# Attention and a ternary feed-forward on one core: first two batches without DMA transposes, weight loads on another queue, normalisations on GpSimd, a new table of times

## The reference

```python
# x, ctx: (16, 128, 1024)
x = x + tanh(g_xattn) * xattn(layernorm(x), ctx, ctx)
x = x + tanh(g_ffn) * ffn(layernorm(x))

def xattn(q, k, v):           # 8 heads of 64, per batch
    qh, kh, vh = Wq.T @ q, Wk.T @ k, Wv.T @ v        # (512, 1024)
    qh = softmax(qh, over a head's 64 rows) * 64 ** -0.5
    kh = softmax(kh, over the 1024 columns)
    context = kh @ vh.T        # 64 x 64 per head
    out = Wo @ (context.T @ qh) + bo
    return out / norm(out over the 128 rows) * g * sqrt(128)

def ffn(h):                    # h (2048, 1024), weights (2752, 1024)
    gate, up = h @ tern(w_gate).T, h @ tern(w_up).T
    return (gate * up) @ tern(w_down).T

def tern(w):                   # scale needs all of w first
    scale = mean(abs(w)); return round(clip(w / (scale + 1e-5), -1, 1)) * scale
```

## Time and profile before

| | us |
|---|---|
| median of 3 runs | 1525.23 (1522.23 to 1528.7) |
| the profiled execution | 1532.59 |
| its span, first to last instruction | 1530.7 |
| PE busy | 1356.5 (89%) |
| DVE busy | 948.4 (62%) |
| ACT busy | 643.7 (42%) |
| POOL busy | 313.7 (20%) |
| data moved by DMA | 196.41 MB |

### The profile page before, as it was taken

One profiled execution on the slowest core, in us unless ns is written; L12 is line 12 of the kernel. 1 busy time (PEld: TensorE's weight loads), 2 busy tenths in 40 slices (PEclk: granted clock), 3 DMA queues, 4 the chain that ended last, 5 costly groups with the idle time before them and its releaser, 6 DMA issues.

```text
span 1530.7 us, 23979 instructions
## 1 busy us (share of the span) xinstructions
PE 1356.5 (89%) x9596; PEld 960.9 (63%) x9596; DVE 948.4 (62%) x1495; ACT 643.7 (42%) x971; POOL 313.7 (20%) x233
## 2 busy tenths in 40 slices
PE   4546350978999999999999999999999999999999
PEld 2324220756757875687658765887578857884884
DVE  5777453766766776677676776676667675742220
ACT  4558663565524442434343443434344434330220
POOL 0129441163221112111121112121112121110000
PEclk9768675989999999999999999999999999999999
DMA  9897999977774246544752375435642565212001
GB/s 353 304 264 245 242 180 207 219 165 124 151 167 102 51 97 152 113 81 84 156 119 57 84 138 127 86 92 104 151 90 50 103 145 90 70 29 76 22 1 42
DMA packets 338191, 196.41 MB, mean 128 GB/s; under 512 B 304352, under 2 KB 304480, under 8 KB 338080
## 3 DMA queue, kind: packets, MB, share of 16 engines
q1 hardware_dynamic: 319120, 126.97, 40.9%
q10 hardware_dynamic: 18960, 67.90, 14.1%
HBM read 102.57 MB, written 16.78 MB: 78 GB/s over the span
## 4 chain that ended last, share of the span: by engine, by line
PE 79%; DMA 9%; DVE 5%; issue 4%; SPq 1%; ACT 1%; POOL 1%; ACTq 0%; DVEq 0%; POOLq 0%
PE ps L741 36%; PE ps L766 19%; PE ps L572 7%; PE ps L573 7%; PE ps L574 7%; DMA kT<-k 4%; DMA cx_raw<-in_ctxn 2%; DMA eT<-p 2%; PE ps L713 1%; SPq L512 1%; PE ps L721 1%; DMA qs<-in_wo 1%; DVE qs L1176 0%; DVE q_stat L1182 0%; DVE kT L949 0%
## 5 line engine op out<-in xcount | busy, mean ns | idle before, releaser
L741 PE MATMUL ps<-zT,w_gu 128*128 128x256 f16 x5504 | 626.2, 273 | 0.0
L741 PEld LDWEIGHTS ps<-zT,w_gu 128*128 128x128 fp8e4 x5504 | 539.5, 98 | 83.4
L766 PE MATMUL ps<-w_dn,inter_buf 128*128 128x512 fp8e4 x1376 | 307.7, 379 | 0.2 <-DVE inter_buf L949 0.2
L766 PEld LDWEIGHTS ps<-w_dn,inter_buf 128*128 128x128 f16 x1376 | 134.7, 99 | 154.2 <-issue 0.4
L1293 POOL TENSOR_TENSOR qs<-qs,q_stat 128x1024 f32<-128x1024 f32 x64 | 127.3, 1988 | 383.7 <-DVE q_stat L1187 383.7
L778 ACT ACTIVATE gate<-ps 128x256 f32<-128x256 f32 (+1 forms) x176 | 67.2, 382 | 310.2 <-PE ps L741 308.9
L1233 DVE SCALAR_TENSOR_TENSOR gate<-ps,gate 128x256 f32<-128x256 f32 (+1 forms) x176 | 74.0, 421 | 181.3 <-ACT gate L778 180.0
L949 DVE TENSOR_TENSOR inter_buf<-gate,inter_buf 128x256 f16<-128x256 f32 (+1 forms) x176 | 82.3, 467 | 66.9 <-ACT inter_buf L778 66.8
L572 PE MATMUL ps<-kT,cT 128*128 128x256 f16 x256 | 74.1, 289 | 52.1 <-DMA kT<-k 46.9
L889 ACT ACTIVATE qs<-qs,l_used 128x1024 f32<-128x1024 f32 x64 | 73.2, 1143 | 96.7 <-DVE qs L1176 96.7
L1299 POOL TENSOR_TENSOR rsv<-ssv,cst 128x4 f32<-128x4 f32 x32 | 45.4, 1418 | 323.6 <-DVE ssv L1203 323.6
(11 more groups left out here) (134 smaller groups left out, 1788.2 us busy)
## 6 DMA issues: line engine op xcount, KB each, us to landing
inter_buf<-in_gate_w ACTq DMA_DIRECT2D x20, 512.0 KB, 10.2
inter_buf<-in_up_w ACTq DMA_DIRECT2D x20, 512.0 KB, 5.7
w_dn<-in_up_w ACTq DMA_DIRECT2D x20, 512.0 KB, 6.0
w_dn<-in_gate_w ACTq DMA_DIRECT2D x19, 512.0 KB, 10.9
w_dn<-in_down_w ACTq DMA_DIRECT2D x18, 512.0 KB, 6.8
inter_buf<-in_down_w ACTq DMA_DIRECT2D x17, 512.0 KB, 5.1
cx_raw<-in_ctxn SPq DMA_DIRECT2D x16, 512.0 KB, 4.5
q_raw<-in_x SPq DMA_DIRECT2D x16, 512.0 KB, 4.7
```

The costliest lines, as they stand in the source:

```text
L741: last = nc.tensor.matmul(ps[:, j % 2, s * T:s * T + T], w_gu[:, w, k, :], zT[:, h, k, :], start=(k == 0 and h == 0), stop=(k == NC - 1 an ...
L766: mm = nc.tensor.matmul(ps[:, hf, :], lhs, w_dn[:, j, hf * 512:hf * 512 + 512], start=(u == 0), stop=(u == total - 1))
```

## The change

- For batches 0 and 1 the context is loaded a second time, already transposed in memory (`ld_ctxT`, an input `ctxt` that holds it so), and scaled and split on ACT and DVE (`ct_hi`, `ct_lo`) in place of `turn_c`; `z` is turned by PE (`zt`) and split out of PSUM (`zt_hi`, `zt_lo`) in place of `z_hi`, `z_lo`, `turn_z`.
- `wload` moves from ACT to SP; `ld_ctx`, `ld_xq`, `ld_xr` move from SP to ACT.
- A buffer `stage_c` of two slots is added, and a branch for slots above 10; `STAGES` itself is not in the diff.
- `q32`, `q_lo` and `z` move from DVE to POOL.
- The factor E_SCALE moves from a DVE instruction on the sums of q (`q_sized`) into the copies `e_hi`, `e_lo`, `qf_hi`, `qf_lo`.
- Of the sums of weights ACT takes four in five instead of two in three.
- `zT_in` becomes one semaphore for each batch of a group.
- All times of the table are new, with the second group now written out of its own. The chunks of down are summed from 1434 on instead of 1678.

```diff
-FFN_FROM = (1969, 3625, 5231)
-EVERY = 1607
+FFN_FROM = (1489, 3382, 5019, 6625)
+EVERY = 1606
...
-    "turn_c": [[159], [675], [1274], [1948], [2754], [3481], [-885], [-143]],
-    "kt": [[168, 181, 252, 265], [685, 709, 772, 792], [1284, 1504, 1517, 1635], [1909, 2075, 2088, 2161],
+    "ld_ctxT": [[0], [312], [], [], [], [], [], [], [], []],
+    "turn_c": [[], [], [1581], [2168], [2642], [3141], [3917], [4756], [-1088], [-276]],
+    "kt": [[139, 152, 201, 216], [558, 713, 833, 881], [1594, 1607, 1654, 1685], [2044, 2246, 2320, 2333],
...
-SUM_ACT = [c for c in range(IC) if c % 3 != 0]
+SUM_ACT = [c for c in range(IC) if c % 5 != 0]
...
+        stage_c = sb("stage_c", [P, 2, CH])
...
+            if s > 10:
+                return stage_c[rows, s - 11, cols]
...
-            def ld_ctx(i, _):
-                if i:
-                    wait(sp, c_lo_s, i)
-                    sp.dma_start(cx_raw[:, :], ctx_rows[rows_of(i), :]).then_inc(ctx_in, 16)
...
+            def wload(m, c, n):
+                kind = STAGED[n][0]
+                s = SLOT[n]
+                if n == 0:
+                    sp.wait_ge(ctx_in, 16)
+                wait_stage_done(sp, BEFORE[n])
...
+                    sp.dma_start(v, src[:, c * CH:c * CH + v.shape[1]]).then_inc(s_load_w[s], 16)
...
+            def zt(i, _):
+                if i == 0:
+                    pe.wait_ge(s_small, 80)
+                wait(pe, z_ready, i + 1)
+                wait_banks(proj_free[PROJ])
+                for k in range(NC):
+                    last = nc.tensor.transpose(ps[:, PROJ + k // 4, (k % 4) * P:(k % 4) * P + P],
+                                               z32[:, k * P:k * P + P], ident[:, :])
+                last.then_inc(zt_ready, 1)
+                proj_free[PROJ][0] = (zt_lo_s, i + 1)
...
+            def ld_ctx(i, _):
+                if i:
+                    wait(act, c_lo_s, i)
+                    nc.scalar.dma_start(cx_raw[:, :], ctx_rows[rows_of(i), :]).then_inc(ctx_in, 16)
...
+            def ld_xr(i, _):
+                if i < GB + BY_PE:
+                    wait(act, zt_ready, i - 1)
+                else:
+                    wait(act, zT_in[i % GB], 16 * ((i - BY_PE) // GB))
+                nc.scalar.dma_start(xb[:, i % 2, :], x_rows[rows_of(i), :]).then_inc(xr_in[i % 2], 16)
...
+            def ct_hi(i, _):
+                wait(act, ctxT_in, 16 * (i + 1))
+                wait(act, c_scaled, 2 * i + 1)
+                wait(act, ctxk_done, 2 * i)
+                scaled(flat(cT[:, 0, :, :]), ct_raw[:, :], c_per[:, i % 2:i % 2 + 1]).then_inc(ct_hi_s, 1)
...
+            def zt_hi(i, _):
+                wait(act, zt_ready, i + 1)
+                o = (i % GB) * P
+                copy(zT[:, 0, :, o:o + P], pair(PROJ).rearrange("p (k t) -> p k t", k=NC)).then_inc(zt_hi_s, 1)
...
-                nc.vector.tensor_scalar(q_stat[:, u % 2, 1, :], q_stat[:, u % 2, 1, :], 1.0 / E_SCALE, None,
-                                        ALU.mult).then_inc(q_sized, 1)
-                wait(dve, q_sized, NU * i + u + 1)
...
+            def q32_(i, _):
+                wait(pool, rstd1, i + 1)
+                nc.gpsimd.tensor_scalar(q_raw[:, :], q_raw[:, :], mv[:, 0:1], mv[:, 3:4], ALU.subtract,
+                                        ALU.mult).then_inc(q32, 1)
...
+            def q_lo_(i, _):
+                wait(pool, q_hi_s, i + 1)
+                wait(pool, qt_ready, NU * i)
+                minus(qn16[:, 1, :], q_raw[:, :], qn16[:, 0, :]).then_inc(q_lo_s, 1)
...
+            def z(i, _):
+                wait(pool, rstd2, i + 1)
+                wait(pool, x2_ready, 2 * i + 2)
+                nc.gpsimd.tensor_scalar(z32, xb[:, i % 2, :], mv2[:, 0:1], mv2[:, 3:4], ALU.subtract,
+                                        ALU.mult).then_inc(z_ready, 1)
```

More of the change, by code:

```diff
@@ L181, in planned @@
 def planned(kind, i):
-    if i < 3 * GB:
+    if i < 4 * GB:
         return PLAN[kind][i]
-    return [group_start(i // GB - 1) + t for t in PLAN[kind][3 * GB + i % GB]]
+    return [group_start(i // GB - 1) + t for t in PLAN[kind][4 * GB + i % GB]]
 def attention_times(i):
@@ L388, in gated_attention_ffn @@
         ln2, rstd2, z_ready = sem("ln2"), sem("rstd2"), sem("z_ready")
-        z_hi_s, z_lo_s, zT_in = sem("z_hi_s"), sem("z_lo_s"), sem("zT_in")
+        z_hi_s, z_lo_s = sem("z_hi_s"), sem("z_lo_s")
+        zT_in = [sem(f"zT_in{b}") for b in range(GB)]
         gu_ready, gate_copied, inter32, inter_hi, inter_lo = (
@@ L550, in st_out @@
                 sp.dma_start(out_rows[rows_of(i), hf * 512:hf * 512 + 512], fin[:, hf, :]).then_inc(out_stored[hf], 16)
-            program({"consts": consts, "ld_ctx": ld_ctx, "ld_xq": ld_xq, "ld_xr": ld_xr, "turn_c": turn_c,
+            program({"consts": consts, "wload": wload, "turn_c": turn_c,
                      "turn_k": turn_k, "turn_q": turn_q, "turn_z": turn_z, "st_x2": st_x2, "reload": reload,
@@ L728, in gu @@
                     if j == 0:
-                        wait(pe, zT_in, 16 * GB * (g + 1))
+                        if g * GB < BY_PE:
+                            wait(pe, zt_lo_s, GB * (g + 1))
+                        else:
+                            for b in range(GB):
+                                wait(pe, zT_in[b], 16 * (g + 1 - BY_PE // GB))
                         if g == 0:
@@ L906, in yev @@
                 if hf == 0:
-                    wait(act, z_lo_s, i)
+                    if i - 1 < BY_PE:
+                        wait(act, zt_ready, i)
+                    else:
+                        wait(act, z_lo_s, i - BY_PE)
                 if i == 0:
@@ L939, in i_hi @@
                     copy(inter_tail[0:TAIL, :], gate[0:TAIL, j % 2, :]).then_inc(inter_hi, 1)
-            program({"gains": gains, "l_hi": l_hi, "wload": wload, "wsum": wsum, "wsign": wsign, "c_hi": c_hi,
+            program({"gains": gains, "l_hi": l_hi, "ld_ctx": ld_ctx,
+                     "ld_ctxT": ld_ctxT, "ld_xq": ld_xq, "ld_xr": ld_xr, "ct_hi": ct_hi, "zt_hi": zt_hi, "wsum": wsum, "wsign": wsign, "c_hi": c_hi,
                      "kexp": kexp, "k_hi": k_hi_, "kf_hi": kf_hi, "cc_hi": cc_hi_, "m_hi": m_hi, "q_hi": q_hi_,
@@ L1051, in cscale @@
                 wait(dve, c_lo_s, i - 1)
+                if i > 1:
+                    wait(dve, ct_lo_s, min(i - 1, BY_PE))
                 wait(dve, k_exp, PAIRS * (i - 1))
@@ L1306, in x2a @@
                 nc.gpsimd.tensor_tensor(v, v, y, ALU.add).then_inc(x2_ready, 1)
+            def z(i, _):
[3 more added lines that the diff above has]
+                                        ALU.mult).then_inc(z_ready, 1)
             program({"consts": consts, "wquant": wquant, "rstd1": rstd1_, "rstd2": rstd2_,
-                     "qnorm": qnorm, "rs": rs, "x2a": x2a})
+                     "qnorm": qnorm, "q32": q32_, "q_lo": q_lo_, "z": z, "rs": rs, "x2a": x2a})
 def kernel(**inputs):
@@ L1329 @@
         "ctxn": f["ctx_4096"],
+        "ctxt": f["ctx_4096"][:BY_PE].transpose(0, 2, 1).reshape(BY_PE, NC, P, P).transpose(0, 2, 1, 3),
         "wq": f["L0_xattn_Wq"].T,
```

278 lines of the change are left out of this document (143 added, 135 removed), and 72 rows, old and new, of tables (DOWN_AT, GU_AT, PLAN, QUANT_AT).

## The result

The changed kernel takes **1473.49 us**, median of 4 runs (1470.57 to 1474.99); the kernel before takes 1526.95, median of 4 (the three of the table ahead and one more). The ratio is 0.9652, 95% interval [0.9624, 0.9681]. The forecast was 1451 in 1418 to 1500. The profiled execution of the changed kernel took 1473.63 us with a span of 1471.6; the forecast span was 1456.4.

The account below looks back on a forecast made before the run. PE bounds the kernel from 467 us on; before that, DMA transposes beside weight loads delay it. Lags 5 + 6 + 4 + 17 + 25 = 57 on 1399.4 give span 1456.4, then + 1.9 - 7.4 = 1451 us, range 1418 to 1500.

Parts of the forecast that it names:

- one sign that the prediction had named for being wrong: After the second group: the 161.9 us period grows, a new stall in the new order, five times over.
- Start, 5 (2 to 8): Kernel start, through wo and prod: path unchanged, so it stays 5 us behind the table.
- Quantisations, 6: Before the first feed-forward group: little table time from free slot to quantisation, POOL's full load included; 6 us (2 to 10).
- down's first sum, 4: First down sum, due 1.3 us after its load may issue, though a load takes 4.9 or more: 4 us (3 to 6).
- Turns of slot 10, 17: End of the down weights: slot 10's four refills at 7.4 us each against 12.7 in the table, 17 us late.
- Transposes of the first group, 25: Fourteen transposes of batches 2 and 3 beside 44 down loads in one queue: 25 us, lower clock included.
- Normalisations on POOL, 0: After 467 us: POOL's added work (1.12 us twice and 1.9 a batch) is hidden, costing nothing.
- 1058: Second group's start to the last matmul: 1060.5 us in the present kernel less 2.6; 3.2 follow to the span's end.
- From span to time, 1.9 - 7.4: Span to median time: add 1.9 us for the profiled execution, subtract 7.4 for its excess over the median.
- Rival 1: Transposes stay as slow among weights as now, 70 to 75 instead of 25: lag 105, 1499 us; chance 0.16.
- Rival 3: Before the first group POOL sets the pace, slow quantisations and moved work adding 12: 1463 us; chance 0.12.
- Rival 4: SP blocked by its own order, transposes waiting behind eleven slots' loads: 88 us on top, 1539 us; chance 0.05.

Follow-up runs that it names:

- e2: Changed kernel with z and q32 moved back from POOL to VectorE, 11 slots: 1464.85 us.
- e3: Changed kernel with 13 stage slots instead of 11, so that stage_c is used: 1451.14 us.
- e1: Changed kernel with z alone moved back from POOL to VectorE: 1468.16 us.
- e5: Kernel before with only the weights' loads issued by SyncE instead of ScalarE, own table, 11 slots: 1458.74 us.
- e12: Kernel before with ScalarE issuing the transposes and the second load of x too, beside the weights' loads: 1535.99 us.
- e7: Changed kernel with 13 stage slots and z and q32 back on VectorE: 1435.46 us.
- e4: Changed kernel with the weights' loads back on ScalarE and the loads of context and x back on SyncE: 1488.55 us.
- e13: Kernel before with the weights' loads issued by SyncE and 13 stage slots instead of 11: 1461.11 us.
- e8: Changed kernel with z and q32 kept on POOL but computed as product, then subtraction of a second scalar from memory: 1481.55 us.
- e9: Changed kernel with z on POOL as subtraction, then multiplication by a constant, to price the form only: 1473.78 us, one run.
- e10: Changed kernel with 13 stage slots and z and q32 on POOL as product and sum, without subtraction: 1428.41 us.

## Why the prediction was right, and where it missed

The direction and the place of the gain were right, and the sum reached its goal before the second group: 57 forecast, 57.2 measured. That it did so to 0.2 us is luck: two of its terms are off by some 7 us each, in opposite directions. The time of 1473.49 us is inside the stated 1418 to 1500, but outside the forecast's own 1430 to 1470, and one sign that the prediction had named for being wrong did come: the period grew.

- *Start, 5 (2 to 8).* 10.5 at the first ctxk, over its upper bound. Of this, wo on the path of the constants makes some 3: it lands at 14.8 us, beside the 1.5 MB that ScalarE issues at once, where it landed at 11.6 in the kernel before. The rest was not traced. (The first weight load goes out at 7.7 us, 2.8 later than before, where I had 1.6.) That q32(0) takes 3.8 us on POOL is not the reason: the lag is 9.8 in e2 too.
- *Quantisations, 6, down's first sum, 4.* The lag at the first feed-forward matmul is 14.7 against 15 (5 + 6 + 4), so these two came to about 4. That matmul is at 163.6, in the 155 to 175 given, and the first transpose goes out at 174.3, none before the 165 given.
- *Turns of slot 10, 17.* The last four loads of the slot go out at 278.5, 285.8, 292.6 and 299.0, its last sign ends at 305.95: turns of 7.3, 6.8, 6.4 and 7.0 where I had 7.4. The lag of the signs grows from 34.5 to 49.2 over them, 14.7. The tile fin in 270 to 307 us, which answers to the earlier trace rows:

```profile
L1345 POOL TENSOR_SCALAR fin<-fin,wthr x5: 1116/1118/1941, 276.2 to 303.6; 128x1024 f32<-128x1024 f32 x5
L906 ACT ACTIVATE w_dn<-fin,cst x5: 1147/1148/1148, 277.4 to 304.8; 128x1024 fp8e4<-128x1024 f32 x5
...
DMA to landing us min/median/max: 2.8/3.6/4.9
```

  e3 shows the mechanism right and the price low: without these turns the lag is 24 less at the second group, not 17, since slots are short in the down weights before the last four too (lag 12 less at down's first matmul).
- *Transposes of the first group, 25.* What is left: 57.2 - 14.7 - 14.7 = 28, short slots in it. The transposes' median landing there is 4.4 us (eT) to 5.9 (zT), in the 3 to 10 given. In e3 the lag grows from 15.7 to 33.2 with transposes and without the slot turns, 17.5 at most for the transposes, so 25 was too much by some 7, as 17 for the slots was too little by 7.
- *Normalisations on POOL, 0.* **This is the step that failed.** "POOL gains 1.12 twice" took the length of a multiply-and-add for a subtract-and-multiply, 1.12 us where 3.79 were measured. At 3.79 us each POOL has 47 us of work in 163 and is still far from full, so the argument by busy time ("hidden") would have stood. But z lies in a chain of waits that goes through ScalarE's order, and 12.3 us of the span's 15.2 come from there (e2; with z alone 11.5, e1). PE's waits shown above name gmul with 5.2 us of this; the other waits that go with z on VectorE were not followed one by one. The other 3 are in "1058": without POOL's part 1063.9 us pass from the second group to the end of the span, not 1061.2.
- *From span to time, 1.9 - 7.4.* Measured +1.9, so 7.3 us of the time's miss. The 7.4 was how much the one profiled execution of the kernel before was slower than its median, and nothing said that the changed kernel's would be too.

Rival 1, that transposes stay slow since one engine's issue is as good as another's, had 0.16. It asked for a lag of 105 at the second group, and 57.2 was measured. Its reason fails too: in e5 and e12 the transposes of c take 6.8 and 8.1 us in one queue, 22.6 in two (24 to 160 us). The Trainium skill (DMA: Bandwidth & Descriptors, "Issuing engines are not separate DMA queues") says that issuing from several engines saves only issue time. The runs differ: here each issuer has its own queue (q1, q10), and whether the transposes share the loads' queue changes their landing by 15 us each and, with ScalarE freed, the time by 70. The measurement decides. Its rule of turns packet by packet in "Queues, rings and completion order" fits that difference, and the packet counts of the earlier trace rows agree with it.

Rival 3 (POOL sets the pace before the first group) is right in its mechanism and wrong in its price. From 110 to 163 us POOL is busy 51.92 of 53.00 us (its column is the fifth of the busy times), and just ahead of the first feed-forward matmul PE waits 8.9 us for z of batch 1 on POOL (ysq is its tile, L667 the turn of z by PE):

```profile
110.00:163.00 53.00, 25.82 (x119) 17.52 (x116) 23.35 (x37) 42.25 (x44) 51.92 (x44) 0.65 0.89 323
```
```profile
PE ps L667 <- POOL ysq L1391: 8.9, 1, 8.9
```

But the 12 us more that it asked for did not come: the lag there is 14.7, as in the sum, whose 6 held POOL's full stretch. Rival 4 (a transpose waits 14.3 us plus 2.4) did not come: the longest landing in the first group is 11.8 us, of one turn_k issued at 195.6 us.

What I had not seen is where the gain comes from. I put the slow transposes down to two queues, but counted the gain as that of the whole change. By runs, all with 11 slots unless said:

| kernel | us |
|---|---|
| before | 1529 |
| + weights' loads on SyncE (e5) | 1458.7 |
| + the rest of the change but z and q32 on POOL: context twice, z turned by PE, small loads on ScalarE, new table, q_lo on POOL (e2) | 1464.9 |
| + z and q32 on POOL, the changed kernel | 1473.5 |
| e2 with 13 slots (e7) | 1435.5 |

Two parts seem to cure the same illness: in the changed kernel, which has four transposes fewer, the shared queue is worth some 6 us at most and not 70 (e4). No run takes the four transposes out by themselves. The new table, with the parts that share it, looks drawn for more slots than it got: with 11 it loses 6 us to the old one (e2 against e5), with 13 it wins 23 (e7 against e5), while the old one gains nothing from 13 (e13). Its second group is due 24.3 us sooner (338.2 against 362.5), and it starts 25.7 sooner with 13 slots (366.5 against 392.2) and 6.4 later with 11 (398.6). What each of the parts in the third row brings by itself was not tried, since they share one table.

Left open: why the second group comes 5.1 us later in e1 than in the changed kernel (3.2 in e2). 3.0 and 1.8 us of this are there at the first feed-forward matmul. VectorE has more to do before it in both, but no wait was found that carries the difference, and with 13 slots it is not there (e7).

## What to carry to other kernels

Where small-packet transfers run beside large ones, look first at whether they share a queue: putting both in one, on an engine that does not compute, was worth more than all the rest here. The issuer counts too: with the one queue on ScalarE the transposes were as fast and the time was not better. A load on the first path stays off that queue. Price an instruction by a row with the same operations, not only the same shape and engine; and where an engine is idle four fifths of the time, ask who waits in order behind its result before calling more work there hidden. When a written-out order is changed together with a resource, test the resource alone: a table is only as good as the number of buffers that it assumes.

## What the runs showed of the hardware

- GpSimd's tensor-scalar on 128x1024 float32 takes 3.74 to 3.87 us (means) with a subtraction among its two operations, whether that stands first or second and whether one scalar comes from memory or two (changed kernel, e8, e9). With product and sum and two scalars from memory it takes 1.21 and 1.29 us (e10), and with one 1.12 us in the median of the earlier trace rows. VectorE takes 0.81 us for the subtraction and product.
- A transpose of 2048 packets of 256 B beside 4 KB loads lands in 22.6 us (20.2 to 24.2) from another queue than the loads' and in 6.8 to 8.1 us (medians; 4.5 to 12.3) from the queue of the loads, in 24 to 160 us, where the DMA engines are busy 0.88 to 0.93. In e4's first group, beside the loads of the down weights and again in another queue, kT lands in 6.9 us (median).
- Issuing such a transpose holds the issuing engine's queue instruction for 1.3 to 9.5 us, a 512 KB load for 0.33 us in the median (ScalarE in e12).
